# Last attention of a four-layer kernel: scores on 32-row tiles, and the causal mask as products on TensorE

## What is computed

```python
    y = jnp.einsum('bse,ef->bsf', x, W1) + b1
    y = y.reshape(B, S, H, -1).transpose(0, 2, 1, 3)
    q, k, v = jnp.split(y, 3, axis=-1)
    w = jnp.einsum('bhqd,bhkd->bhqk', q, k) / dk      # dk = sqrt(8)
    mask = jnp.tril(jnp.ones((S, S), dtype=x.dtype))
    w = w * mask - NEG_BIG * (1.0 - mask)
    w = jax.nn.softmax(w, axis=-1)
    attn = jnp.einsum('bhqk,bhkd->bhqd', w, v)
    attn = attn.transpose(0, 2, 1, 3).reshape(B, S, E)
    return jnp.einsum('bse,ef->bsf', attn, W2) + b2
```

## Time and profile before

| | |
|---|---|
| median of 3 runs | 1695.23 us (1692.74 to 1699.27) |
| the profiled execution | 1706.63 us, its span 1704.9 us |
| mean granted TensorE clock | 0.952 of full speed |
| busy over the span: TensorE / VectorE / ScalarE / GpSimd | 87% / 74% / 64% / 50% |
| last attention, first score to last exp | about 1354 to 1688 us of the span |

### The profile page before, as it was taken

How to read it: one execution, slowest core, us unless ns; L and a number is a source line. 1 busy time by engine, 2 the same in 40 slices (tenths; PEclk the granted TensorE clock), 3 DMA queues, 4 the chain that set the end, 5 groups by cost and what they waited for, 6 DMA issues and landing times. The chain is left out here.

```text
span 1704.9 us, 29946 instructions
## 1 busy us (share of the span) xinstructions
PE 1490.4 (87%) x11248; PEld 1197.3 (70%) x11248; DVE 1260.4 (74%) x2770; ACT 1089.9 (64%) x2122; POOL 857.1 (50%) x798
## 2 busy tenths in 40 slices
PE   6999999999999999899848888845999379998997
PEld 4788887888788887687737676834788256666675
DVE  6999999999999999435461677589433887777772
ACT  4888888888888888455445565632444456666665
POOL 4556576667666666720363744624666632233211
PEclk9999999999999999999779999957999699999999
DMA  3656666656666565300044000040465200000000
GB/s 94 124 103 115 106 120 100 120 108 114 115 108 103 99 105 106 87 1 1 18 137 129 26 2 2 2 133 1 112 148 109 64 1 1 2 2 2 2 2 26
DMA packets 334417, 117.09 MB, mean 69 GB/s; under 512 B 281008, under 2 KB 326096, under 8 KB 334144
## 3 DMA queue, kind: packets, MB, share of 16 engines
q1 hardware_dynamic: 323664, 101.54, 29.2%
q0 software_dynamic: 8496, 12.59, 3.4%
q10 hardware_dynamic: 2112, 1.05, 0.2%
HBM read 37.53 MB, written 10.49 MB: 28 GB/s over the span
## 5 line engine op out<-in xcount | busy, mean ns | idle before, releaser
L2135 ACT ACTIVATE ET_a<-PS 128x256 f32<-128x256 f32 (+2 forms) x512 | 220.5, 499 | 114.8 <-PE PS L2028 72.9
L771 POOL TENSOR_TENSOR dl<-XN,dh 128x1024 f16<-128x1024 f32 x86 | 184.9, 2150 | 155.2 <-DVE D L743 79.7
L205 PE MATMUL PS<-xh,yh 128*128 128x512 f32 x512 | 215.5, 421 | 6.6 <-ACT XNT L608 3.8
L206 PE MATMUL PS<-xl,yh 128*128 128x512 f32 x512 | 204.0, 398 | 0.0
L207 PE MATMUL PS<-xh,yl 128*128 128x512 f32 x512 | 202.8, 396 | 0.0
L608 ACT ACTIVATE G<-PS,nm 128x1024 f32<-128x1024 f32 x128 | 143.0, 1117 | 53.4 <-DVE nm L693 37.9
L608 ACT ACTIVATE XNT<-PS,nm 128x1024 f32<-128x1024 f32 x128 | 143.1, 1118 | 52.3 <-DVE nm L693 41.0
L687 DVE TENSOR_REDUCE nm<-PS 128x1 f32<-128x1024 f32 x128 | 156.6, 1223 | 15.7 <-PE PS L207 13.8
L689 DVE TENSOR_REDUCE nm<-PS 128x1 f32<-128x1024 f32 x128 | 156.0, 1219 | 4.7 <-PE PS L207 1.0
L205 PE MATMUL PS<-dth,xnh 128*128 128x256 f16 x512 | 141.0, 275 | 12.0 <-DVE zl L697 12.0
L2323 DVE CUSTOM_DVE_ANT_0 PS<-PS,mk 128x256 f32<-128x256 f32 (+3 forms) x256 | 128.2, 516 | 30.6 <-PE PS L2007 30.2
(11 more groups left out here) (461 smaller groups left out, 4091.1 us busy)
## 6 DMA issues: line engine op xcount, KB each, us to landing
e_wg<-in_WgT SPq DMA_DIRECT2D x16, 256.0 KB
e_wu<-in_WuT SPq DMA_DIRECT2D x16, 256.0 KB
e_wd<-in_WdT SPq DMA_DIRECT2D x16, 256.0 KB
dth<-dh SPq DMA_TRANSPOSE x128, 3.2
dtl<-dl SPq DMA_TRANSPOSE x128, 3.2
m_x_rows<-m_xs SPq DMA_DIRECT2D x1, 1472.0 KB, 4.9
m_xs<-m_x_rows SPq DMA_DIRECT2D x5, 256.0 KB, 4.8
m_y_rows<-m_xs SPq DMA_DIRECT2D x5, 256.0 KB, 2.3
```

The source lines that it names most:

```text
L205: e.matmul(o, l[0], r[0], start=start, stop=False)
L206: e.matmul(o, l[0], r[1], start=False, stop=False)
L771: e.tensor_tensor(self.dl[:, g % 4, :], self.D[g % 3], self.dh[:, g % 4, :], SUB).then_inc(*self.d_low.up(g))
L2135: e.activation(dst, src, ACT.Exp, scale=self.SC, bias=0.0).then_inc(*self.ex.up(it))
```

## The change

Scores of the last attention contract over one head's 32 partitions alone, on 32-row tiles of the array (`tile_position=(32 * hh, 0)`), straight from tiles KA and QA that hold all four heads. The spreads of K (ScalarE and GpSimd) are gone. For odd j the score uses copies KZ and QZ, in which the two halves of the partitions are exchanged (64 partitions each, by DMAs on SyncE's queue, 2 for each `project` and 2 small ones for each `max`), so that the row and the column score of step j and those of step j+1 stand in four different row groups: hh, hh-1, hh+2, hh+1. The mask is added by TensorE: for each part with a diagonal block, rows and columns (8 and 8 of the 24 parts of a head), a bf16 product of the identity with a 128 x 128 mask (0 or -1e10) accumulates onto the score, on the full array, after each odd step. So VectorE takes every row maximum with a plain reduction, and GpSimd's cut is gone. Order: lag 70 instead of 63, `AV_AT` (4, 10) instead of (0, 4), `misc` at new places, rows before columns in a step, and the parts of rows and columns in another order. GpSimd has nothing left in the stage but the work of `lead`.

```diff
-        self.AV_AT = (0, 4) if kind == 3 else (11, 12)
-        self.lag = 63 if kind == 3 else 70
+        self.AV_AT = (4, 10) if kind == 3 else (11, 12)
+        self.lag = 70
...
             if hh == 0 and 1 <= n <= self.NQ:
-                m += [("max", n - 1, c) for c in range(2)]
-            if n + 1 < self.NQ and hh in (1, 2):
-                m += [("project", n + 1, w_, hh - 1) for w_ in (1, 0)]
+                m += [(1, ("max", n - 1, 0)), (5, ("max", n - 1, 1))]
+            if n + 1 < self.NQ:
+                m += {1: [(1, ("project", n + 1, 1, 0)), (8, ("project", n + 1, 0, 0))], 2: [(0, ("project", n + 1, 1, 1))],
+                      3: [(1, ("project", n + 1, 0, 1))]}.get(hh, [])
             if x - 7 >= 1 and (x - 7) % 2 and x - 7 < NH:
-                m += [("give", x - 7)]
+                m += [(8, ("give", x - 7))]
...
+        def masks():
+            q.wait_ge(w.ready, "maskT")
+            for o, i, sig, it in late:
+                e.matmul(o, w.identb[:, :], w.mk[:, i, :], start=False, stop=True).then_inc(*sig.up(it))
+            late.clear()
...
                 i, c0, c1, first = self.rparts[j]
                 wd = max(c1 - c0, 256)
-                t = e.matmul(o[:, 0:wd], qs[:, 128 * i:128 * i + 128], kh[:, c0:c0 + wd], start=True, stop=True)
+                if n and j % 2:
+                    self.swap_landed(q, ("project", n, 1, (c0 + wd - 1) // 512))
+                    self.swap_landed(q, ("project", n, 0, i // 4))
+                    hh, qs, kh = (hh + 2) % 4, self.QZ[:, n % 3, :], self.KZ[:, n % 3, :]
+                r = slice(32 * hh, 32 * hh + 32)
+                t = e.matmul(o[:, 0:wd], qs[r, 128 * i:128 * i + 128], kh[r, c0:c0 + wd], start=True, stop=first, tile_position=(32 * hh, 0))
+                if not first:
+                    late.append((o[:, c1 - c0 - 128:c1 - c0], 0, self.row, it))
+                    return
...
+            if self.kind == 3 and j in self.at and x < self.NH:
+                row(x, self.at[j])
             if m in self.at and 0 <= y < self.NH:
                 col(y, self.at[m])
-            if j in self.at and x < self.NH:
+            if self.kind == 3 and j % 2:
+                masks()
+            if self.kind == 1 and j in self.at and x < self.NH:
                 row(x, self.at[j])
...
-                    e.tensor_tensor_reduce(out=o[:, 0:c1 - c0], in0=o[:, 0:c1 - c0], in1=w.mk[:, 512 - (c1 - c0):512], scale=-1.0,
-                                           scalar=3e38, op0=ADD, op1=MIN, accum_out=dst).then_inc(*self.top.up(it))
+                    e.tensor_reduce(dst, o[:, 0:c1 - c0], AX.X, MAX, negate=True).then_inc(*self.top.up(it))
```

More of the change, by code:

```diff
@@ L1118, in __init__ @@
         ops += ["one"] if kind == 3 else ["bq0", "one"]
-        ops += [("bm", 0), ("bm", 1)] + (["ident"] + [("mask", i, j) for i in range(3) for j in range(2)] if kind == 1 else ["m0", "open", "mask", "m1", "bv"]) + ["va1", "va0"]
+        ops += [("bm", 0), ("bm", 1)] + (["ident"] + [("mask", i, j) for i in range(3) for j in range(2)] if kind == 1 else ["m0", "ident", "mask", "maskT", "m1", "bv"]) + ["va1", "va0"]
         self.ready = k.sig("s_weights", ops)
@@ L1646, in __init__ @@
         self.scratch = None if kind == 3 else self.ET[1][:, :, :].rearrange("p j w -> p (j w)")[:, 0:1024]
-        self.KH = [[sb(f"KH{n}_{i}", [128, 1024], F32R) for i in range(4)] for n in range(3)]
+        if kind == 3:
+            self.KA, self.KZ, self.QZ = [sb(n, [128, 3, 1024], F32R) for n in ("KA", "KZ", "QZ")]
+        else:
+            self.KH = [[sb(f"KH{n}_{i}", [128, 1024], F32R) for i in range(4)] for n in range(3)]
         edge = 64 if kind == 1 else 0
@@ L1721, in __init__ @@
         self.use = use
+        self.swaps = [u for u in use if u[0] in ("project", "max")]
+        self.swapped = [k.sig(f"a_swapped{i}", grid(self.swaps[i::4], range(2)), 16) for i in range(4)] if kind == 3 else None
         self.fifth = [u for (x, j), u in self.misc.items() if x < 5 and self.side_of.get(u) == 5]
@@ L1776, in __init__ @@
         self.av = k.sig("a_values", range(NH))
-        self.cut = k.sig("a_cut", grid(range(NH), range(2)))
+        self.cut = k.sig("a_cut", grid(range(NH), range(2))) if kind == 1 else None
         self.out = k.sig("a_out", range(1, NH, 2))
@@ L1784, in __init__ @@
         self.seen = (self.fin_st, "st")
-        self.ends = [(self.fin_p, 3), (self.fin_a, 3), (self.fin_d, self.fin_d.last), (self.cut, self.cut.last)]
+        self.ends = [(self.fin_p, 3), (self.fin_a, 3), (self.fin_d, self.fin_d.last), (self.cut, self.cut.last) if kind == 1 else (self.ex, self.ex.last)]
         self.bq, self.bm = w.bq, w.bm
@@ L1863, in sp, with swap_landed @@
             self.moe.sp_rows(e, q)
+        if self.kind == 1:
+            return
+        for m, u in enumerate(self.swaps):
+            n, ck = u[1], u[-1]
+            cs = slice(512 * ck, 512 * ck + 512)
+            if m >= 4:
+                self.swap_landed(q, self.swaps[m - 4])
+            q.wait_ge(self.mi, u)
+            if u[0] == "project":
+                src, dst = (self.KA, self.KZ) if u[2] else (self.QA, self.QZ)
+                parts = slice(0, 64), slice(64, 128)
+                if n >= 3:
+                    q.wait_ge(self.col, ("col", 4 * (n - 3) + 3, self.nc_ - 1))
+            else:
+                src, dst = self.QA, self.QZ
+                parts = slice(24, 57, 32), slice(88, 121, 32)
+                self.swap_landed(q, ("project", n, 0, ck))
+            for i in range(2):
+                e.dma_start(f(dst[parts[1 - i], n % 3, cs]), f(src[parts[i], n % 3, cs])).then_inc(*self.swapped[m % 4].up((u, i)))
+    def swap_landed(self, q, u):
+        q.wait_ge(self.swapped[self.swaps.index(u) % 4], (u, 1))
     def pool(self, e, q):
@@ L1875, in pool @@
         else:
[L1876 to L1885, removed]
+            for x in range(4):
+                self.lead.pool_at(e, q, x)
             return
@@ L2027, in col @@
                 wd = max(q1 - q0, 256)
-                t = e.matmul(o[:, 0:wd], kh[:, 128 * jj:128 * jj + 128], qs[:, q1 - wd:q1], start=True, stop=True)
+                if j % 2:
+                    for c in range(2):
+                        self.swap_landed(q, ("project", n, 1, c))
+                        self.swap_landed(q, ("max", n, c))
+                    hh, qs, kh = (hh + 2) % 4, self.QZ[:, n % 3, :], self.KZ[:, n % 3, :]
+                r = slice(32 * hh, 32 * hh + 32)
+                own = q0 == 128 * jj
+                t = e.matmul(o[:, 0:wd], kh[r, 128 * jj:128 * jj + 128], qs[r, q1 - wd:q1], start=True, stop=not own, tile_position=(32 * hh, 0))
+                if own:
+                    late.append((o[:, wd - (q1 - q0):wd - (q1 - q0) + 128], 1, self.col, it))
+                    return
             else:
@@ L2039, in sums @@
             per, et = self.avs[x], self.ET[x % 2]
+            if self.kind == 3:
+                q.wait_ge(self.ex, ("col", x, self.nc_ - 1 if part else max(j for j, c in enumerate(self.cparts) if c[0] == 3)))
+            else:
+                q.wait_ge(self.cut, (x, 1))
             if part == 0:
-                q.wait_ge(self.cut, (x, 1))
                 q.wait_ge(w.ready, "va0")
@@ L2091, in project @@
             high(u, o)
-            spread(u)
+            if self.kind == 1:
+                spread(u)
         def high(u, o):
@@ L2102, in high, with spread @@
             e.activation(hn, o, ACT.Identity, scale=m3[:, w_:w_ + 1], bias=self.bm[:, w_, qd:qd + 1]).then_inc(*self.mi_act.up(u))
-        def spread(u, heads=(0, 2)):
+        def spread(u):
             _, n, w_, ck = u
@@ L2108, in spread @@
                 q.wait_ge(self.mi, u)
-                for hh in heads:
+                for hh in (0, 2):
                     r = slice(32 * hh, 32 * hh + 32)
                     self.k_free(q, n, hh)
[L2112 to L2116, removed]
+                    to = self.KH[n % 3][hh][:, 512 * ck:512 * ck + 512]
+                    e.activation(to[r, :], f(hn[r, :]), ACT.Copy).then_inc(*self.k_act.up(("k", n, ck, hh)))
         def col(x, j):
@@ L2166, in act @@
                 col(y, self.at[m])
-            if j == (6 if self.kind == 3 else 13) and 0 <= x - 6 < self.NH and x % 2:
+            if j == (12 if self.kind == 3 else 13) and 0 <= x - 6 < self.NH and x % 2:
                 take_out(x - 6)
@@ L3409, in sp @@
         self.lead.sp(e, q)
+        self.attn.sp(e, q)
     def pool(self, e, q):
```

84 lines of the change are left out of this document (34 added, 50 removed).

## The result

The changed kernel takes 1757.16 us (median of 4 runs, 1733.84 to 1801.30) against 1694.24 us before, a ratio of 1.037 by these medians; the two quickest of the four runs alone (1733.84 and 1753.43) give 1.029, 95% interval 1.018 to 1.039. Slower, as forecast, but by 63 us where 11 were forecast, and outside both ranges of the prediction (1700 to 1715, and 1674 to 1727). The runs spread by 67 us where those of the kernel before spread by 7, and the time goes with the mean granted clock of TensorE: 1733.8 us at 0.936, 1753.4 at 0.917, 1760.9 at 0.914, 1801.3 at 0.886; in the runs of the kernel before it was 0.950 to 0.955. This spread is the kernel's own, so its runs with a low clock are told of here too.

A forecast was written before the change was run, and what follows sets the result against it. The stage was taken as paced by hand-overs between engines, none full. Edges, a middle of 10.15 us a head and the end summed to +10.3 us: 1695.2 becomes 1705.5, said as 1706; range 1700 to 1715, wider 1674 to 1727.

The forecast's parts named there:

- The sum: Last attention: first row to first column +1, middle +10.4, columns alone +1.6, end -2.7; together +10.3 us.
- C: Rival on scores: tiles' loads or streams don't overlap, 0.2 to 0.5 us more a group; 1728 us and up, chance 0.10.
- The head: Middle of last attention: a head without side work takes 9.25 us instead of 7.73, scores becoming readable in pairs behind masks.
- rival A: Switches between array shapes nearly free and tiles pack well: head about 8.3 us, total 1676 us; chance 0.32.
- the sides: Side work (`max`, `give`, projections) in the last attention: 3.6 us a quad against 8.2 before.
- Scores on tiles: Scores on 32-row tiles, loads overlapping in different row groups: 0.42 us a group of four, 0.32 for two.
- Switches: Tiled to full array and back around masks: 0.10 us in, 0.15 out; twelve new switches, 1.5 us a head.
- Masks: Mask products on TensorE: 16 of 128 columns a head at 0.055 us each, 0.9 us a head.
- Copies: 48 swaps of 2 DMAs on SyncE, costed at nothing; uncovered, one would cost 2.6 us a quad.
- Rival D: The second max's swap arrives late, before column 1: up to 21 us, total 1727 us; chance 0.03.
- ScalarE's relief: Spreads of K and the waits before them leave ScalarE: 4.3 us a quad off that engine.
- the line of the prediction: VectorE's maxima, masked or plain: 0.07 us plus 1.04 ns a column; gain from plain reductions taken as 0.

The follow-up runs named there:

- masks_alone: Kernel before with only the mask moved to TensorE, as a bf16 product on the full array behind each score that needs it; 1721.29 us, ratio 1.014.
- order_copies: order_alone with the spreads of K for quads 3 to 7 made by DMAs from SyncE's queue; 1671.24 us, ratio 0.985.
- order_alone: Kernel before with only the changed order (lag 70, sums at steps 4 and 10, side work moved); full array, spreads and masks as before; 1689.16 us, ratio 0.996.
- rows32: order_alone with each score contracting only 32 rows, each head in its own row group; 1762.77 us, ratio 1.035.
- serial32: order_alone with each score contracting only 32 rows, always in row group 0, so none overlap; 1890.19 us, ratio 1.114.

## Why the prediction was right or wrong

- **The step that failed: every duration was taken at the full clock.** The sum, the rivals and both ends of the range rest on rows at clock 1.00 (the earlier trace rows and the middle stretch of the earlier trace rows), and nothing in them asks what 32-row products do to it. Measured in its place: the half level for some 149 us of the stage, worth about 54 us by the heads of the profiled execution and about 49 of the 63 us by the line through the runs. No rival named it; C, with the nearest time, has another mechanism (tiles that don't overlap), which the starts within 0.01 us refute.
- **The head.** Forecast 40.6 us a quad, measured 40.0 at the full clock. That this is right to 1.5% is in part luck, for two misses cancel. A head without side work was forecast at 9.25 us and took 8.63, nearer to the 8.3 of rival A (kernel after, the chain's second sums, no product of `max`, `give` or `project` between them):

```profile
1647.31 1.29 PE PS L2093 x40
...
1655.94 1.28 PE PS L2093 x40
```

By the same reckoning as before (40.0 less four such heads) the sides take 5.5 us a quad, where 3.6 were forecast and 8.2 were read before.
- **Scores on tiles.** Taken: 0.42 from the start of a group of four to the end of its streams. Measured: 0.43 from the first start to the first mask, with the 0.10 of the switch in it, so 0.1 less.
- **Switches.** Forecast 0.10 in, and 0.15 out ahead of a load. Measured: the pair with 384 columns that starts at 1513.98 has its mask at 1514.36 (0.11 for the load, 0.16 to stream, 0.11 left); after three masks (0.17 by the prediction's 0.055) the next scores start at 1514.63, 0.10 later. Runs of one to four masks have 0.17, 0.23, 0.27 and 0.32 us from their start to the next scores (1512.16, 1513.16, 1514.36, 1516.66), or 0.12 and 0.05 a mask. So some 0.11 in and 0.10 to 0.12 out. The Trainium skill, TensorEngine Tiling (Array Packing), Tiling Modes, is borne out: masks after tiles pay a drain. Rival A (switches nearly free) was wrong.
- **Masks.** Forecast 0.9 us a head; masks_alone shows 0.94 net, all on the path. Right in size; that it all counts on a full array wasn't foreseen.
- **Copies.** Forecast nothing; no wait for a DMA shows in the stage. Rival D was wrong.
- **Order.** I priced it within the new head and at its edges, never by itself; alone it gives 7.9 us back. Tiles and masks together are thus measured against 1689 us, not against 1694.
- **ScalarE's relief.** Forecast that the sides fall by 4.6 us a quad, from 8.2 to 3.6. They fell by 2.7, and order_copies shows the same size for the spreads alone: 37.98 - 35.07 = 2.9 us a quad. In the changed kernel masks and switches took it back.
- **VectorE.** Almost nothing gained from the plain reductions, as taken: two of 384 and 512 columns take 1.06 us from start to start (1519.70 to 1520.76), 1.07 by the line of the prediction, and with the mask 1.12 to 1.16 in order_alone. Its idle time in the second sums was forecast at 2 us; the kernel after shows 1.74:

```profile
1516.92 1.16 DVE L2356 TENSOR_REDUCE top<-PS 128x1 f32<-128x384 f32 x2 [1.74 <-PE PS L2007]
```

## What to carry to other kernels

Before products are cut to fewer rows because the rest of the array only multiplies zeros, ask what holds TensorE's clock: here the zero rows were not waste, and taking them away cost more than all that was freed (rows32 alone is 74 us over order_alone). Price the parts of a combined change one by one, the order too: here the reordering alone was a gain that the other parts buried. Where an engine in the loop only moves data between partitions, an idle DMA queue may do it, if what it needs is a head ahead.

## What the runs showed of the hardware that I had not expected

- With products on 32 of 128 rows the granted clock fell to 0.5 for tens of microseconds with TensorE busy nearly all the time: 0.50 from 1394 to 1834 us in serial32, busy 431 of these 440 us, where 128-row products of the same number and width ran at 0.96 to 1.00 (order_alone). 64 rows lie between (0.75 to 1.00 by stretch from 1394 us on).
- The level isn't fixed by the program: the same stretch of the changed kernel had 0.77 in one profile and 1.00 in another, and its eight times spread from 1733.8 to 1801.3 us. A kernel whose times spread by 4% on one core, while another's spread by 0.4%, is worth a look at the clock first.
- Four fp32r products of 32 rows start within 0.01 us of each other with their weight loads (1518.98 and 1518.99 us, 0.18 each), so loads of 128 columns in different row groups don't queue.
